# Cross-attention and a routed feed-forward on one core: a token-tile loop one pass shorter and in another order

## What is computed

```python
x = x + attention(layernorm(x), ctx, Wq, bq, Wk, bk, Wv, bv, Wo, bo)   # 4 x 2048 tokens of 512, 16 heads of 32, 77 keys
x = x + ffn(layernorm(x))

def ffn(x):                                  # 8 experts, inner width 1024
    w = softmax over the top 2 of x @ emb.T  # 0 for the other six
    keep = cumsum(w > 0 over tokens) <= capacity
    vals, idx = top_k((w * keep).T, capacity)   # per expert; capacity = 8192 tokens / 8 = 1024
    out = relu(x[idx] @ W1.T) @ W2.T * vals
    return zeros.at[idx].add(out)
```

## Time and profile before

| | us |
|---|---|
| median of 3 runs | 1577.38 (1575.84 to 1584.79) |
| profiled execution, its own time | 1584.22 |
| its span, first to last instruction | 1582.5 |
| PE busy / DVE / ACT / POOL | 1380.9 (87%) / 975.1 (62%) / 822.7 (52%) / 701.1 (44%) |
| residual of tile 0 / of tile 63 begins | 151.2 / 822.2 |
| mean granted clock of PE | 0.929 |

### The profile page before, as it was taken

One profiled execution on the slowest core, in us unless ns is written; L12 is line 12 of the kernel. 1 busy time (PEld: TensorE's weight loads), 2 busy tenths in 40 slices (PEclk: granted clock), 3 DMA queues, 4 the chain that ended last, 5 costly groups with the idle time before them and its releaser, 6 DMA issues.

```text
span 1582.5 us, 30761 instructions
## 1 busy us (share of the span) xinstructions
PE 1380.9 (87%) x12330; PEld 793.7 (50%) x12330; DVE 975.1 (62%) x1989; ACT 822.7 (52%) x1374; POOL 701.1 (44%) x655
## 2 busy tenths in 40 slices
PE   7547999999898899986761899999999999999996
PEld 3335777766665566664330644444444444444442
DVE  7687888999677967787336354545445454545431
ACT  3556888878776778875335351423333241515120
POOL 2156877777656656765211414223241415141301
PEclk9668999999898999998775999999999999999998
DMA  6337989988765667777312346465645547473401
GB/s 205 99 109 161 202 213 228 213 206 202 176 162 130 148 142 168 162 189 180 98 55 89 110 120 170 124 156 149 157 145 142 144 123 191 120 187 107 113 24 40
DMA packets 321160, 231.78 MB, mean 146 GB/s; under 512 B 253481, under 2 KB 253865, under 8 KB 321018
## 3 DMA queue, kind: packets, MB, share of 16 engines
q1 hardware_dynamic: 305658, 179.17, 47.2%
q0 software_dynamic: 15360, 50.66, 10.9%
HBM read 121.87 MB, written 50.86 MB: 109 GB/s over the span
## 4 chain that ended last, share of the span: by engine, by line
PE 71%; DVE 15%; issue 4%; ACT 4%; POOL 2%; DMA 2%; SPq 1%; DVEq 0%; POOLq 0%; ACTq 0%
PE ps L1124 22%; PE ps L1138 21%; PE ps L1033 10%; PE ps L963 5%; PE ps L1014 3%; PE ps L1050 3%; DVE ps L1355 3%; DVE sd L1368 2%; DVE sm L1389 1%; DVE x L1411 1%; PE ps L937 1%; PE ps L986 1%; PE ps L1028 1%; PE ps L948 1%; DVE xnT L1348 1%
## 5 line engine op out<-in xcount | busy, mean ns | idle before, releaser
L1124 PE MATMUL ps<-xT,w1s 128*128 128x512 f16 (+1 forms) x1632 | 348.6, 373 | 16.9 <-issue 15.7
L1138 PE MATMUL ps<-w2s,hT 128*128 128x512 f16 x1536 | 332.8, 379 | 0.0
L807 ACT ACTIVATE hT<-ps 128x512 f16<-128x512 f32 (+1 forms) x136 | 77.0, 572 | 388.4 <-PE ps L1124 292.4
L1124 PEld LDWEIGHTS ps<-xT,w1s 128*128 128x128 f16 x1632 | 161.1, 99 | 202.2 <-issue 38.4
L1138 PEld LDWEIGHTS ps<-w2s,hT 128*128 128x128 f16 x1536 | 150.2, 98 | 181.3
L532 POOL TENSOR_TENSOR sd<-sd,rr 128x1232 f32<-128x1232 f32 x64 | 144.1, 2251 | 179.4 <-ACT rr L709 176.7
L963 PE MATMUL ps<-xnT,wqh 128*128 128x256 f16 x1536 | 203.4, 286 | 11.4 <-ACT partq L691 11.2
L1033 PE MATMUL ps<-woh,oT 128*128 128x512 f16 x768 | 208.2, 428 | 2.9 <-POOL oT L520 2.9
L1666 DVE SCALAR_TENSOR_TENSOR hT<-ps,hT 128x512 f16<-128x512 f32 (+1 forms) x136 | 88.0, 657 | 174.3 <-ACT hT L807 115.8
L569 POOL DMA_INDIRECT out_dram<-ys,idx x64 | 71.8, 1122 | 278.2 <-DVE ys L1676 278.2
L538 POOL TENSOR_TENSOR ph<-sd,ph 128x1232 f16<-128x1232 f32 x64 | 162.2, 2535 | 27.9 <-ACT ph L719 27.3
(11 more groups left out here) (202 smaller groups left out, 2054.4 us busy)
## 6 DMA issues: line engine op xcount, KB each, us to landing
xt<-x SPq DMA_DIRECT2D x64, 256.0 KB, 2.8
xr<-x SPq DMA_DIRECT2D x64, 256.0 KB, 3.0
xrow_dram<-x SPq DMA_DIRECT2D x64, 256.0 KB, 2.7
out_dram<-x SPq DMA_DIRECT2D x64, 256.0 KB, 4.2
stage<-w1T SPq DMA_DIRECT2D x8, 2048.0 KB
stage<-w2T SPq DMA_DIRECT2D x8, 2048.0 KB, 8.4
xs<-x SPq DMA_DIRECT2D x62, 256.0 KB, 3.3
wqf<-wq SPq DMA_DIRECT2D x1, 1024.0 KB, 7.0
```

The lines of the kernel that those rows point to most:

```text
L1124: ins = pe.matmul(hb[z][:, 0:wide], w1s[e % 2][:, a, k, ic * P:(ic + 1) * P], xT[:, 4 * b + k, cols], start=(k == 0 and i == 0), stop=(k = ...
L1138: ins = pe.matmul(yb[z][:, :], hT[:, a, k, s * P:(s + 1) * P], w2s[e % 2][:, b, k, :], start=(k == 0 and i == 0), stop=(k == 7 and i == 2))
```

## The change

- The loop begins at h = -8: 72 passes. The softmax pieces come one pass sooner after the scores' place in the output pipeline: s_mm(h + 7), exponentials h + 6, sums and probabilities h + 5, p_T(h + 4). Norm statistics are spread over passes -8 to 33.
- On SP `p_T` stands first in the pass (before the loads), no more behind the stores.
- ACT's `ln1_apply` stands first in the pass, in the start too.
- PE's `invert` stands right behind `o_mm`, DVE's `add_slots` right behind `residual`; `rank` moves from the head of a pass to the tail of the one before.
- POOL's 14 norm steps of a batch fall in one pass (up to 16 steps), not in two (9 each).
- Passes 55 to 63 have orders of their own on ACT and PE: `pv_mm` is first and writes the bank `bA[1]`, which the queries no longer need; `logits` comes one pass later, behind `o_mm`; ACT makes four one-hot steps at the end of the pass. The second weight load moves from pass 54 to 56.

```diff
@@ def xattn_moe
         def stats_at(h):
 
-            if h < 0:
-                return {-9: range(8, 10), -8: range(10, 13), -7: range(13, 16), -6: range(16, 19), -5: range(19, 22),
-                        -4: range(22, 25), -3: range(25, 28), -2: range(28, 30), -1: range(30, 32)}[h]
-            return range(h + 32, min(h + 33, T))
+            if h < 2:
+                return {-8: range(8, 11), -7: range(11, 14), -6: range(14, 16), -5: range(16, 19), -4: range(19, 22),
+                        -3: range(22, 25), -2: range(25, 27), -1: range(27, 29), 0: range(29, 31),
+                        1: range(31, 32)}[h]
+            return range(h + 30, min(h + 31, T))
@@ sync (SP)
-            for h in range(-9, T):
-                load_x(h + 15)
+            for h in range(-8, T):
+                p_T(h + 4)
+                load_x(h + 14)
                 if h >= 1:
                     load_r(h + 4)
+                for t in stats_at(h):
+                    if h == -8 and t >= 10:
+                        load_s(t)
                 for t in stats_at(h + 1):
                     load_s(t)
-                if -8 <= h < -3:
-                    for k in range(5 * (h + 8), 5 * (h + 9)):
+                if -7 <= h < -2:
+                    for k in range(5 * (h + 7), 5 * (h + 8)):
                         values_place(0, k)
...
                 store_x(h)
                 store_o(h)
-                p_T(h + 5)
...
                 if h == 50:
                     load_w(0, 1)
-                if h == 54:
+                if h == 56:
                     load_w(0, 2)
@@ gpsimd (POOL)
-            for h in range(-9, T):
+            for h in range(-8, T):
                 G, half = divmod(h, 2)
+                Q, part = divmod(h + 9, 2)
...
-                if h in (-6, 0, 16, 32):
-                    first = norm_pool({-6: 3, 0: 4, 16: 5, 32: 6}[h])
+                if h in (-5, 2, 18, 34):
+                    first = norm_pool({-5: 3, 2: 4, 18: 5, 34: 6}[h])
...
-                p_norm(h + 6)
+                p_norm(h + 5)
                 steps(first, 4)
                 steps(second, 2)
-                q_lo(G + 5, 2 * half)
+                q_lo(Q, 2 * part)
                 steps(first, 3)
                 o_lo(G + 1, half)
-                q_lo(G + 5, 2 * half + 1)
-                steps(first, 2)
+                q_lo(Q, 2 * part + 1)
+                steps(first, 9)
                 steps(second, 2)
-                p_lo(h + 6)
+                p_lo(h + 5)
@@ o_hi (ACT)
-                act.copy(o_both(G, 0, half), bA[0][:, :])
+                src = bA[1 if 2 * G + half >= TAIL + 2 else 0][:, :]
+                act.copy(o_both(G, 0, half), src)
...
@@ scalar (ACT)
-            for h in range(-9, T):
+            for h in range(-8, TAIL):
...
+                ln1_apply(h + 12)
+                s_min(h + 6)
+                tx_hi(h + 11)
...
+                s_exp(h + 6)
+                steps(ones, 1)
+                r_scale(h + 5)
+                q_hi(Q, 2 * part)
...
+                o_hi(G + 1, half)
+                t2_copy(h)
+                q_hi(Q, 2 * part + 1)
+                steps(ones, 1)
+                p_hi(h + 5)
+            for h in range(TAIL, T):
...
                 o_hi(G + 1, half)
+                s_min(h + 6)
+                s_exp(h + 6)
+                r_scale(h + 5)
                 t2_copy(h)
+                p_hi(h + 5)
+                steps(ones, 4)
@@ tensor (PE)
-            for h in range(-9, T):
+            for h in range(-8, TAIL):
+                G, half = divmod(h, 2)
+                Q, part = divmod(h + 9, 2)
+                H = inverted_at(h)
+                o_mm(h)
+                if H is not None:
+                    invert(H)
+                tx(h + 11)
+                q_mm(Q, 2 * part)
+                pv_mm(G + 1, half)
+                s_mm(h + 7)
+                t2(h)
+                q_mm(Q, 2 * part + 1)
+                logits(h)
+                if h in (21, 37, 53):
+                    rank((h - 21) // 16)
+            for h in range(TAIL, T):
                 G, half = divmod(h, 2)
                 H = inverted_at(h)
-                if h in (22, 38, 54):
-                    rank((h - 22) // 16)
+                pv_mm(G + 1, half, 1)
                 o_mm(h)
-                tx(h + 12)
-                q_mm(G + 5, 2 * half)
-                pv_mm(G + 1, half)
-                s_mm(h + 8)
-                t2(h)
+                s_mm(h + 7)
+                if h > TAIL:
+                    logits(h - 1)
                 if H is not None:
                     invert(H)
-                q_mm(G + 5, 2 * half + 1)
-                logits(h)
+                t2(h)
+            logits(T - 1)
@@ vector (DVE)
-            for h in range(-9, T):
+            for h in range(-8, T):
...
                 if h in (22, 38, 54):
                     route = ranking((h - 22) // 16)
+                    steps(route, 1)
...
-                s_sum(h + 6, 0)
+                s_sum(h + 5, 0)
                 residual(h)
-                s_sum(h + 6, 1)
+                if H is not None and h < TAIL:
+                    add_slots(H)
+                s_sum(h + 5, 1)
                 steps(route, 1)
-                s_recip(h + 6)
-                tx_lo(h + 12)
+                s_recip(h + 5)
+                tx_lo(h + 11)
...
                 ln2_aggr(h)
+                if H is not None and h < TAIL:
+                    next_batch(H)
                 steps(route, 1)
                 for t in stats_at(h):
                     ln1_stats(t)
-                if h in (-7, -1, 15, 31):
-                    steps(norm1({-7: 3, -1: 4, 15: 5, 31: 6}[h]), 9)
+                if h in (-6, 1, 17, 33):
+                    steps(norm1({-6: 3, 1: 4, 17: 5, 33: 6}[h]), 9)
...
-                score(h + 8)
-                if H is not None:
+                score(h + 7)
+                if H is not None and h >= TAIL:
                     add_slots(H)
                     next_batch(H)
```

More of the change, by code:

```diff
@@ L42 @@
 RMAXN = 16
+TAIL = 55
 PAIRS = [(g, c) for g in range(4) for c in range(GK * g // P, (GK * (g + 1) - 1) // P + 1)]
@@ L989, in s_mm, with pv_mm @@
                 ins.then_inc(S["s"], 1)
-            def pv_mm(G, half):
+            def pv_mm(G, half, n=0):
                 if not 0 <= G < NG:
```

41 lines of the change are left out of this document (17 added, 24 removed).

## The result

The changed kernel takes 1509.5 us (median of 4 runs, 1500.3 to 1517.0); the kernel before took 1576.6 beside it. The ratio is 0.9582, 95% interval 0.9542 to 0.9621: 66 us, or 4.2%, faster. The forecast was 1503 in a range of 1482 to 1533. The profiled execution is the slowest of the four, 1517.0 us with a span of 1515.0. In one experiment (label e11_both_back) five of ten executions, the profiled one among them, lie more than 1.5% above its fastest and are left out of its ratio.

What follows compares the result with a forecast made beforehand. PE was taken as bound in passes 0 to 14, DVE in 15 to 23, none from 24, where PE waits for acc. Terms -14 + 2 - 12.5 - 17 - 13 - 19.5 = -74 us: 1503 us, range 1482 to 1533.

Steps and rivals of the forecast that it cites:

- the forecast's own 1488 to 1518: Whole kernel: the spread of the forecast time itself, without the rivals; chance 0.65.
- Start, -14: First exponential to first residual: one pass less and transposing transfers issued sooner save 14 us, bounds -6 and -21.
- Passes 0 to 14, +2 with the next stretch: Passes 0 to 23: same engines stay the bound, possible late transfers cost 2 us, bounds 0 and +8.
- Passes 15 to 23, about 0: First router batch: DVE stays the bound, nothing gained; costed with passes 0 to 14 at +2 us together.
- Passes 24 to 30, -12.5: No wait for acc, 9.5 us a pass: 66.5 for 79.0 us, bounds -8 and -13.
- Passes 31 to 39, -17: Second router batch: DVE's work of 90.7 us at share 0.96 gives 94.5 for 111.6, bounds -8 and -22.
- Passes 40 to 53, -13: Eight passes at 9.5 us and six by DVE's share: 134 for 147.2 us, bounds -7 and -15.
- Passes 54 to 62, -19.5: Last passes: new order breaks the single chain, transposing transfers come next; 83.6 for 103.4 us, bounds -8 and -30.
- Behind pass 63, 0: What follows pass 63 is unchanged and starts earlier; the later second weight load costs 0.
- The rule on the order of descriptors: Transfers of tiles 55 and 61 sit behind weight loads, each 4 to 6 us later: sum some 7 us higher, 1510.
- The rival on the slower side: P·V of half 0 waits for late transfers in every even pass, 4.7 us each, 127 us over 27: 1630; chance 0.05.
- The rival of ACT or DVE as the next bound: Middle passes: another engine takes PE's place, half of the 42.5 us is lost: 1524; chance 0.13.

Runs made afterwards that it cites:

- e11_both_back: Changed kernel with DVE's addition behind the scores and PE's table product behind the turning again; ratio to the kernel before 0.9947, median over all ten executions 1571.5 us.
- c_before_again: The kernel before run once more, unaltered, for its lengths by stretch; 731.9 us behind pass 63.
- c_after_again: The changed kernel run once more, unaltered; ratio to the kernel before 0.9572.
- e6: Changed kernel with SP's 25 placements of the first values one pass earlier; ratio to the kernel before 0.9551, first residual at 136.2 us.
- e7: Changed kernel with POOL's normalisation and low part of the probabilities each in two instructions of half width; ratio to the kernel before 0.9495.
- e8: Changed kernel with POOL's halves, first values a pass earlier and later batches' norm steps over two passes; 1472.0 us, ratio to the kernel before 0.9452.
- e10: As e8 but with POOL's two long operations in quarters instead of halves; 1470.1 us, ratio to the kernel before 0.9439.
- e1: Changed kernel with DVE's addition to acc behind the scores again, PE's table product left behind the output product; ratio to the kernel before 1.0037.
- e2: Kernel before with only the addition part: table product behind output product, addition behind residual up to pass 55, ranking a pass ahead; ratio 0.9742.
- e3: Changed kernel with the order of its last passes on PE and ACT undone; ratio to the kernel before 0.9716, passes 54 to 62 at 98.4 us.
- e9: Kernel before with POOL's two long operations in halves and nothing else; ratio to the kernel before 1.0012.
- second group: Four kernels run on one chip: c_after_again, the changed kernel with later norm steps over two passes, e6 and e7; 742.7 to 752.6 us behind pass 63.
- the third: Group of four kernels run on one chip: c_before_again, e8, e9 and e10; 731.9 to 732.9 us behind pass 63.

## Why the prediction was right, and where not

- **The number.** 1509.5 for 1503, inside the forecast's own 1488 to 1518. Errors of opposite signs helped: summed up to pass 63, I forecast -74 and the traces show -56; behind it they show -11.5, which is not the change's. The second profiles of the two kernels (c_before_again, c_after_again) have 65.9 us between their residuals of pass 63, which is the whole of the measured 66: the first pair understates it, by passes 0 to 14 of the kernel before (139.1, then 144.7 us) and 15 to 23 of the changed one (101.6, then 99.0).
- **Start, -14: measured -7.6.** DVE's busy time fell by 8.7 us (63.5 to 54.8), as summed, and the waits of ACT for the transfer went. The step that failed is the one on the transposing transfers ("at the head of SP's pass, one pass and some 12 us sooner"): it did not ask what they are put ahead of. The placements of the values, now a pass nearer to their use and behind the transfer, are late next. e6 moves them back and gives 6 to 7 us: with that the term is -15.
- **Passes 0 to 14, +2 with the next stretch: measured +1.0.** SP's lag did not grow into waits of P·V. Passes 1 and 3 are 0.6 and 0.8 us longer, beside the statistics and norm steps that now fall there.
- **Passes 15 to 23, about 0: measured +10.9, in later runs +4.7 to +8.5.** The largest miss. The sentence that failed is "the same engines stay the bound, so nothing is gained": nothing is gained, but DVE is the bound, and its work is not a constant. It grew by 6.5 us with the same instructions, because more of them now start beside POOL's long ones (blocked time 10.4 to 16.5 us). e7 takes the stretch back to 91.3 us, e8 and e10 (which spread the norm steps too) to 90.1 and 89.4, and so shows the cause; the rest of the 10.9 is PE's wait and the clock behind it, largest in pass 19. The rows for it were in the trace of before (42.3 us in all), and I hadn't looked at the spread of one form's duration.
- **Passes 24 to 30, -12.5: measured -13.0.** Right in place and size (e1, e2).
- **Passes 31 to 39, -17: measured -13.3.** I took DVE's work as 90.7 us; it was 93.81, of which 19.4 were blocked time, 3.6 more than before. DVE's share, 0.95, was as forecast. With halves it is 85.5 us and the stretch 90.6, the -21 that lay inside my bounds.
- **Passes 40 to 53, -13: measured -10.5.** The same in small: 12.1 us blocked for 7.9; e7 has 133.2, I had forecast 134.
- **Passes 54 to 62, -19.5: measured -23.5.** Right mechanism (e3: 18.5 for the order). PE's P·V waits for a transfer in every second pass, as said (4.3, 3.1 and 3.9 us in passes 56, 58 and 60); I had the clock low in two output products, and it was 0.85 on the mean.
- **Behind pass 63, 0:** right (c_before_again).
- **The rule on the order of descriptors.** The transfer issued 4.8 us behind the first weight load landed in 7.5 us, the longest between 385 and 690 us, where the median is 6.0; the one issued 6.8 us behind the second took 5.7, inside the 4.8 to 6.6 of its four neighbours. By the rule as weighed (the Trainium skill, DMA: Bandwidth & Descriptors, section on queues, rings and completion order) each would have been 4 to 6 us late. The first row leans its way by 1.5 us and nobody waited there; on the second P·V of pass 58 waited, but it shows no delay; the measured durations decide, and the sum rightly went by the rows.
- **The rival on the slower side** (transfers late in every even pass) did not occur: no wait of P·V for a transfer between pass 0 and 54. The rival of ACT or DVE as the next bound came true for DVE alone and in router passes alone.

What stays open: why the parts interact. The addition's place is worth 41 us alone and 71 on top of the rest; the rest alone is worth nothing (e1: +0.4%, e11: -0.5%, or +0.1% over all its executions), though its start and last passes gain over 20 us. The traces say where: passes 15 to 23 (+5 to +8), 31 to 39 (+4 to +7) and 40 to 53 (+15), in the last with the clock at 0.93 for 0.99. Up to pass 50 the stalls there are as long as before or 0.1 us longer, but in pass 52 they are 4.3 and 4.2 us for 1.5, and that pass alone is 6 us longer; why the addition is so late there was not found. Which executions lose the clock behind a stall of 1.65 us, the runs don't tell; that they do so by chance fits e9 with its two shorter executions of twelve, but was not shown.

## What to carry to other kernels

Before costing a move on a busy engine, compare the longest and the shortest duration of each of its small forms (the median can itself be a blocked one): where they differ by the length of another engine's instruction, the order decides the work, and cutting that long instruction in two can be a cheap remedy (it gained 12 us here, and nothing in the kernel before). When a producer is moved nearer to its use, list everything that stands on the same queue, not only the transfer that was late. A small stall that repeats in every pass is worth more than its length, since the clock may fall behind it: 2.9 us a pass in e9, behind a stall of 1.65.

## What was not expected of the hardware

- A DVE operation of 128x32 elements took 0.16 us alone and up to 2.56 us beside a POOL instruction of 2.52 us, until that one's end, and 1.11 beside one of 1.22. The addition with one operand in PSUM was spared each time (0.19 to 0.22 us in 22). The cast that starts 3 to 9 ns ahead of POOL's instruction went either way: 2.56 us in five profiles and 0.17 in three.
- The same stall of 1.65 us was followed by the full clock in passes 40 to 46 of both executions of the kernel before, and by half the clock in passes 40 and 42 of the kernel before with halves, where it added 2.9 us a pass.
- The part behind pass 63, nearly the same instructions in the kernel before and the changed one (588 of DVE in both), took 732 to 760 us: 742.7 to 752.6 in the four kernels of the second group, and within 1 us of each other in the four of the third. A comparison of two profiles can carry such a difference as if it were the change.
